# Half 0's choice of experts inside attention's last octet, and between pairs of masks in the fifth layer

## The reference

```python
x = x + 0.5 * ffn(layernorm(x));   x = x + attention(layernorm(x))
x = x + 0.5 * ffn(layernorm(x));   x = x + 0.5 * moe(x)
x = x + linear_attention(x);       x = x + 0.5 * moe(x)

# moe: 16 experts, each token goes to its two best
probs = softmax(x @ Wr + br);  topk_w, topk_idx = top_k(probs, 2);  topk_w /= sum(topk_w)
h = gelu(layernorm(x @ W1[e] + b1[e]) * g1[e] + be1[e]);  y = h @ W2[e] + b2[e]
out = sum over the two chosen experts of topk_w * y
```

## Time and profile before

| | us |
|---|---|
| median of 3 runs (lowest, highest) | 658.87 (654.27, 664.81) |
| the profiled execution | 658.0 |
| its span, first to last instruction | 656.2 |
| PE busy | 514.2 (78%) |
| DVE busy | 480.3 (73%) |
| ACT busy | 325.0 (50%) |
| POOL busy | 146.4 (22%) |

### The profile page before, as it was taken

The page is one execution under the profiler, slowest core; times in us unless marked ns, Lnnn a source line. Parts: engine busy times, 40 slices in busy tenths (PEclk is TensorE's granted clock), DMA queues, the critical chain, the costliest instruction groups (busy, mean ns, idle before and its releaser), DMA issues.

```text
span 656.2 us, 9335 instructions
## 1 busy us (share of the span) xinstructions
PE 514.2 (78%) x2975; PEld 278.1 (42%) x2976; DVE 480.3 (73%) x1332; ACT 325.0 (50%) x640; POOL 146.4 (22%) x193
## 2 busy tenths in 40 slices
PE   6687949999998999888735899697797863899710
PEld 3352312222322222234433677484555452677500
DVE  6977978788888998558883756858788976555712
ACT  2355517666766677775311587634242111578600
POOL 3000030000000000000077603554000076602645
PEclk8886969999999899988865799969699865799955
DMA  8106549303000000000315443411000015263422
GB/s 278 43 1 149 93 110 158 126 1 126 2 1 2 1 1 2 2 2 2 128 55 175 131 124 86 117 49 33 1 1 0 1 46 167 69 189 90 138 63 72
DMA packets 54037, 46.55 MB, mean 71 GB/s; under 512 B 5862, under 2 KB 46246, under 8 KB 53734
## 3 DMA queue, kind: packets, MB, share of 16 engines
q1 hardware_dynamic: 33382, 29.23, 16.4%
q0 software_dynamic: 4224, 8.59, 4.4%
q10 hardware_dynamic: 16384, 8.13, 4.4%
HBM read 24.94 MB, written 20.60 MB: 69 GB/s over the span
## 4 chain that ended last, share of the span: by engine, by line
PE 47%; DVE 23%; issue 10%; POOL 7%; ACT 6%; DMA 5%; SPq 2%; POOLq 0%; ACTq 0%; DVEq 0%
PE ps L679 7%; PE ps L651 7%; PE ps L669 7%; PE ps L1124 4%; POOL rows_in L1016 4%; PE ps L1104 4%; DVE arena L726 3%; ACT arena L1176 2%; PE ps L1085 2%; POOL arena L1041 2%; PE ps L1112 2%; SPq L627 2%; DMA arena<-arena 2%; DVE arena L1685 1%; PE ps L1122 1%
## 5 line engine op out<-in xcount | busy, mean ns | idle before, releaser
L726 DVE TENSOR_REDUCE arena<-ps 128x1 f32<-128x512 f32 x256 | 162.0, 684 | 27.4 <-PE ps L651 26.7
L786 ACT ACTIVATE arena<-ps 128x512 f32<-128x512 f32 x256 | 136.8, 601 | 74.8 <-PE ps L669 74.1
L651 PE MATMUL ps<-arena 96*128 96x512 bf16 x256 | 98.9, 396 | 7.5 <-DVE arena L726 6.4
L669 PE MATMUL ps<-arena 99*128 99x512 bf16 x256 | 95.7, 389 | 9.7 <-DMA arena<-arena 8.4
L1016 POOL DMA_INDIRECT rows_in<-xl,route x64 | 62.2, 972 | 155.9 <-DVE route L972 137.3
L1041 POOL DMA_INDIRECT arena<-rows_out,route x64 | 60.8, 950 | 96.5 <-DMA rows_out<-arena 68.5
L679 PE MATMUL ps<-arena 128*32 128x512 f32 x512 | 69.9, 618 | 1.3 <-ACT arena L786 0.7
L669 PEld LDWEIGHTS ps<-arena 99*128 99x128 bf16 x256 | 24.6, 98 | 88.0 <-ACT arena L786 59.1
L797 POOL CAST arena<-arena 128x16 bf16<-128x16 f32 x8 | 1.6, 197 | 236.1 <-issue 144.2
L1214 DVE TENSOR_REDUCE arena<-arena 128x4 f32<-128x512 f32 (+1 forms) x32 | 21.2, 664 | 36.6 <-ACT arena L1166 36.6
L1176 ACT ACTIVATE arena<-ps,route 128x128 f32<-128x128 f32 x124 | 46.7, 460 | 2.3 <-PE ps L1112 2.2
(11 more groups left out here) (272 smaller groups left out, 851.2 us busy)
## 6 DMA issues: line engine op xcount, KB each, us to landing
arena<-rows_in SPq DMA_DIRECT2D x28, 256.0 KB, 4.6
rows_out<-arena ACTq DMA_DIRECT2D x28, 256.0 KB, 2.4
rows_in<-zerob SPq DMA_DIRECT2D x2, 1920.0 KB, 7.2
att_parts<-arena SPq DMA_DIRECT2D x12, 256.0 KB
arena<-att_parts SPq DMA_DIRECT2D x12, 256.0 KB, 9.2
arena<-in_consts SPq DMA_DIRECT2D x2, 1024.0 KB, 5.8
arena<-att_parts SPq DMA_DIRECT2D x14, 128.0 KB, 7.9
x<-in_x SPq DMA_DIRECT2D x4, 256.0 KB, 3.4
```

The lines of the kernel that those rows point to most:

```text
L651: pe.matmul(ps[:, bank, :], a_qs[0:96, b, h, j * P:(j + 1) * P], a_ks[0:96, b, h, keys * 512:(keys + 1) * 512], start=True, stop=True).the ...
L669: pe.matmul(ps[:, score_bank(n), :], a_ks[0:99, b, h0 + h4, i * P:(i + 1) * P], a_qs[0:99, b, h0 + h4, half * 512:(half + 1) * 512], start ...
L726: nc.vector.tensor_reduce(a_nm[:, k % 2, o % 2, k // 2:k // 2 + 1], ps[:, bank, :], AX.X, ALU.max, negate=True).then_inc(a.mpu, 1)
L786: nc.scalar.activation(a_p[:, n % 16, :], ps[:, score_bank(n), :], ACT.Exp, scale=0.25).then_inc(a.ex, 1)
```

## The change

It moves work; almost nothing is added or removed. Four places:

1. In the last octet the ffn of half 0 comes one step earlier on PE and 4 exponentials earlier on ACT; raw and logits of m3[0] come into steps 61 and 62 of attention; the count of m3[0] comes between the last values and `turn_out`. On DVE `centre_experts` goes ahead of the waiting `out_add`, and all of `moe_vector_gap` of m3[0] behind the norm of half 0, ahead of the last octet's copy and `out_add`. The logits of m3[0] get bank 4.
2. Behind the last copy DVE does the first five steps of m3[0]'s slots, and the rest in turn with half 1's norm. Nothing of m3[0] is left between half 1's mix and half 1's ffn add.
3. On ACT the gate of m3[0] goes ahead of half 1's norm.
4. In the fifth layer `states` becomes a generator; the norm of half 0 for the sixth layer runs in turn with half 1's `states`, ahead of half 1's first mask; the gap of m5[0] stands between masks 1 and 2, all its slots between masks 3 and 4 (before: gap in two parts around mask 3, slots behind mask 6). PE's raw, logits, count, turn_bases and scales of m5[0] move to match.

```diff
             values(NSC // 4 - 1)
+            summed(pe)
             turn_out(NO - 1)
...
             in_last_octet(dve, vs, lambda: out_add(NO - 2))
             out_copy(NO - 1)
+            copied()
             out_add(NO - 1)
...
             for t in range(TB):
                 l1.scores(t)
+                routing(2 * t - 1)
                 if t:
                     l1.values(t - 1)
                 if t == 6:
                     l1.project(0)
-                routing(t)
+                routing(2 * t)
...
-            l1.states()
-            l1.mask(0)
             dve.wait_ge(l.y, 2)
             norms = Chain(norm_vector_stats(dve, vs, after, 0, False))
-            for _ in range(12):
+            for _ in range(4):
                 vs.advance(norms)
+            vs.finish_both(Chain(l1.states()), norms)
+            l1.mask(0)
             l1.mask(1)
-            for _ in range(12):
-                vs.advance(norms)
+            vs.finish(Chain(moe_vector_gap(dve, vs, m5[0])))
             l1.mask(2)
-            vs.finish(norms)
-            gap = Chain(moe_vector_gap(dve, vs, m5[0]))
             l1.mask(3)
-            for _ in range(7):
-                vs.advance(gap)
+            vs.finish(Chain(moe_vector_slots(dve, vs, m5[0])))
             l1.mask(4)
-            vs.finish(gap)
             l1.out_in(0)
             l1.mask(5)
             l1.mask(6)
-            vs.finish(Chain(moe_vector_slots(dve, vs, m5[0])))
...
-            if step == 56:
+            if step == 55:
                 ffn_tensor_k(pe, f2, 0)
-            if step == 58:
+            if step == 57:
                 ffn_tensor_r(pe, f2, 0)
-            if step == 60:
+            if step == 59:
                 ffn_tensor_v(pe, f2, 0)
+            if step == 61:
+                raw_tensor(pe, 0, 0, lambda g: pe.wait_ge(f2.added, 2 * B + g + 1))
+            if step == 62:
+                pe.wait_ge(a.done, NO - 1)
+                moe_tensor_logits(pe, m3[0])
...
             norm_vector_xt(dve, n2, 0)
             ffn_vector_mix(dve, vs, n2, f2, 0)
+            centre_experts(dve, vs)
             add()
-            centre_experts(dve, vs)
             ffn_vector_add(dve, vs, f2, 0)
             vs.finish(Chain(norm_vector_stats(dve, vs, n3, 0, False)))
+            vs.finish(Chain(moe_vector_gap(dve, vs, m3[0])))
...
-            att_vector(dve, vs, vector_between(vs), vector_in_last_octet)
-            dve.wait_ge(s_set, 8)
+            slots = Chain(moe_vector_slots(dve, vs, m3[0]))
+
+            def behind_last_values():
+                dve.wait_ge(s_set, 8)
+                for _ in range(5):
+                    vs.advance(slots)
+            att_vector(dve, vs, vector_between(vs), vector_in_last_octet, behind_last_values)
             norms = Chain(norm_vector_stats(dve, vs, n2, 1, False))
-            for _ in range(10):
+            for _ in range(4):
                 vs.advance(norms)
-            vs.finish_both(norms, Chain(moe_vector_gap(dve, vs, m3[0])))
+            vs.finish_both(slots, norms)
             ffn_vector_mix(dve, vs, n2, f2, 1)
-            vs.finish(Chain(moe_vector_slots(dve, vs, m3[0])))
             ffn_vector_add(dve, vs, f2, 1)
...
-            att_tensor(pe, tensor_in_attention, tensor_in_first_octet)
-            raw_tensor(pe, 0, 0, lambda g: pe.wait_ge(f2.added, 2 * B + g + 1))
-            pe.wait_ge(a.done, NO)
-            moe_tensor_logits(pe, m3[0])
+            att_tensor(pe, tensor_in_attention, tensor_in_first_octet, lambda pe: moe_tensor_count(pe, m3[0]))
+            moe_tensor_turn_bases(pe, m3[0])
             keep_clock(pe, FILL_BANK, 6)
             norm_tensor(pe, n2, 1)
-            moe_tensor_count(pe, m3[0])
```

29 lines of the change are left out of this document (16 added, 13 removed).

## The result

The changed kernel takes 653.78 us (median of 20 runs, 651.63 to 655.97), the kernel before beside it 660.15 (20 runs, 652.38 to 664.81 and one of 1164.47). The ratio, which leaves out the slow runs of the kernel before, those over 1.5% above its fastest, is 0.9925, 95% interval 0.9904 to 0.9946: 4.9 us, or 0.75%, faster, and the same by the bound of 2%. Forecast were 647.0 us, 11 less than before. Most lines of the changed kernel lie two further on than those of before, the others none to eight (L1879 is L1879 still, masks are L1691 for L1685, `add` is L1706 for L1700).

The account below looks back on a forecast made before the run. No engine bounds the whole; the two mixtures' entries wait for half 0's rows, and half 1's count comes next. Fourth layer -6.0 and sixth -5.0 make -11.0 from 658.0: 647.0 us; forecast's own range 643.5 to 650.5, wider range 641.5 to 655.5.

Parts of the forecast that it names:

- Half 1's chain is left 2.7 us late.: Fourth layer's entry: half 1's count ends at 345.9, groups begin there instead of at 352.54, gaining 6.6 us.
- The +3.8 at `out_add`: Last octet: half 0's logits, gap, count and slot steps make `out_add` end at 311.4 instead of 307.58.
- The +0.8 for the norm in turn: Fourth layer: half 1's norm, taking turns with half 0's slots, needs 9.0 us instead of 8.2.
- The -1.9 for the slots that left the ffn: Fourth layer: half 0's slots no longer stand between half 1's mix and ffn add, giving back 1.9 us.
- I count +0.6: Fourth layer's groups: POOL's memset holds a DVE tensor_scalar about 1.2 us; net cost 0.6, bounds 0 and 2.5.
- I take what an entry gains as gained at the end of the program.: Both mixtures: the PE-led groups' pitch does not depend on their start, so entry gains last, unless half 1 is late.
- I take no change: Fifth layer: half 1's `add` lands at 533.5 to 534.5 against 533.79, so the sixth layer's groups gain 5.2 us.
- a sign of being wrong: Profile afterwards: half 1's `add` more than 2 us later against the stage's start would show the forecast wrong.
- at about 521.8 instead of 519.8: Fifth layer: when mask 4, which the values of half 1's tile 4 need, was expected to come.
- rival 2: Fifth layer: clock sinks in new waits, half 1's last tiles slip 3 to 5 us; 651.5; 0.25 with small stalls.
- Rival 3: Last octet: late DVE holds PE at raw, attention ends later; needs a 12 us stall, 660 at 17 late; chance 0.04.
- it costs nothing: Fourth layer: POOL's sends beside half 1's norm and mix cost 0, with two to four microseconds of slack.

Follow-up runs that it names:

- chip 11: Chip of the second kind; changed kernel with half 0's fourth-layer sends held until half 1's last ffn add, against the kernel before: 752.29 us, 1.0276.
- chip 3: Chip of the second kind; the changed kernel as it is, against the kernel before on the same chip: 740.88 us, 1.0127.

## Why the prediction was wrong

The direction was right, and so was the mechanism at the entries: both waits for rows went, half 1's count became the last wait in both, and 653.8 lies inside the range. The size was not: 4.9 us, and 3.4 between the traces, where 11.0 were counted. The step that failed most is the one that carried the entries' gain unchanged to the end of the program; behind it come three terms of the sum that were too small. All of this is read from traces of the first kind of chip; no run varied one of these terms there.

- **"Half 1's chain is left 2.7 us late."** It is 4.2 late, so the entry gave 5.3 in place of 6.6. The +3.8 at `out_add` was right to 0.05 us. The +0.8 for the norm in turn was nearly right for DVE (done at 320.68, 4.9 late where 4.6 were counted) and not for the chain: ACT applies its half of the norm, ends at 321.34, and PE's transposes come 5.5 us later than before (321.43 for 315.90), not 4.6. Then ten filling matmuls, 2.92 us before, take 4.34 at the lower clock behind the longer idling, and the key projection waits for their end: 0.7 more. The -1.9 for the slots that left the ffn was right (6.1 late at the output product, 4.4 at the add).
- **"I count +0.6" for the memset.** It cost 1.5 (from -5.9 to -4.4 over that unit). The held tensor_scalar took 1.60 us and ended with the memset at 376.2, the reduce ahead of it its usual 0.69, as the rule that the prediction takes from the Trainium skill (SBUF — State Buffer, section "Who interferes with whom") has it. It was held 1.4 us, not 1.2, and PE then waited 1.30 for it, so the 0.2 of slack wasn't there. The saved 0.39 was set against it in the wrong place: it belongs to the third unit, two ahead, where the gain does rise from 5.2 to 5.8.
- **"I take what an entry gains as gained at the end of the program."** This is the step that failed most. At the ends of both runs of groups PE's clock was lower than before, 0.67 for 0.91 and 0.72 for 0.97, and 1.9 and 1.2 us went there. Before, eight output matmuls of a group still took 1.16 us, the upper level, at 423.15 and 620.93; now they take 2.08, the lower, at 419.53 and 616.51. The second trace on such a chip repeats it (0.64 and 0.70), so it seems to belong to the changed kernel, as far as one trace of before beside two of after can tell. The prediction had weighed the clock only where the groups begin, in attention's last steps and between masks 3 and 4. At the groups' start it did rise, 0.82 for 0.74 from 352 to 380, and the first unit gained 6.3 where the start had gained 5.3. Why it falls at the end was not tested.
- **"I take no change" for half 1's last add.** It came 0.9 later by the clock on the wall and 2.4 later in its stage, more than the 2 us that the prediction itself had named as a sign of being wrong, so the fifth layer gave 3.0 us and not 5.2. The slots came 5.8 earlier in the stage where 6.3 were counted. The cause was a misread row: mask 4 was said to come "at about 521.8 instead of 519.8", but 519.80 is the start of masks 5 and 6 before, and mask 4 ran there at 515.50. It runs at 520.84 now, 5.3 later by the clock on the wall and 6.8 in its stage, so tile 4's values wait 3.79 us for it and come 4.8 later (522.10 for 517.27). Not all of it is made up by the masks without slots between them. States and norm in turn also made PE's transposes wait 2.17 us at 498.42, and its four scores at 524.10 took 2.08, at the lower level, where four took 1.13 before (519.72). That is rival 2's mechanism, at 2.4 us where it had 3 to 5.
- Added up along the table, what is missing is 1.3 (the fourth layer's start) - 1.0 + 0.4 (first units) + 0.9 (memset) + 1.9 (clock) + 1.0 (half 0's way through the linear attention, which no reading explained) + 2.0 (the fifth layer, counted at 5.0) - 0.2 + 1.2 (clock) + 0.1 = 7.6, the 11.0 less 3.4.
- **Rival 3** (slower by a stall of 12 us in the last octet) didn't come at raw. But a stall of 16 us beside half 1's last tiles goes with most of the 9 us by which the change is slower on five chips of six, and the prediction had none with that cause: it dismissed sends beside half 1's work in one sentence, "it costs nothing", from rows of one chip. On that kind of chip nothing speaks against the sentence: from half 1's key projection to its count it is 19.6 us beside the sends, and 19.85 on chip 11 with the sends held back to 334.74, behind the last add. On the second kind it is wrong: the same way takes 28.8 us beside the sends (chip 3).

## What to carry to other kernels

When two chains meet at one point, taking the later one forward wins only up to the other, and everything that the move adds to the other chain, its engines in turn and its clock fills, counts in full. A gain at the entry of a long stage is not yet one at its end: read the granted clock there too, before and after. And work that is made to run beside indirect DMAs should be timed on more than one chip before it is kept: here the same edit gave 0.75% on one, nothing that can be told from zero on a second of its kind, and took 1.3% on another.

## What the runs showed of the hardware

Two kinds of chip, or of surroundings of a chip, ran the kernel before in 655 and in 731 to 735 us. The instructions themselves hardly differ: in the changed kernel DVE is busy 475.7 us for 477.6, PE 539.0 for 519.1, at a clock of 0.81 for 0.86. Most of the 80 us are waits and pauses beside POOL's indirect DMAs, in the kernel before 10% of the chain (74 us of 739) alone with no releaser in the trace. They set in 11 to 15 us behind the first of a run of sends and end 2 to 3 us behind the last, and eight fewer sends of 1.26 us, 10.1 us in all, took 11.2 us off the wait beside them (4.57 for 15.76).
